# Where TensorE computes six value products ahead of the scores loop

## Chip, cores and metric

The kernel runs on one core of a Trainium2 chip. The metric is the device time of one execution in microseconds (us). Several executions are timed, and one is profiled. Engines are named as in the profile: PE is TensorE's matmul, PEld its weight load, DVE VectorE, ACT ScalarE, POOL GpSimd, and SP the engine that issues most DMAs.

## The reference

A decoder layer on x (2048 x 256) and a context of 1601 x 256, all float32:

```
x = layernorm(x + linear_attention(x))            # 8 heads of 64; softmax of q over the head, of k over the tokens
x = layernorm(x + cross_attention(x, context))    # 16 heads of 16: softmax(Q K^T / 4) V, then Wo; biases on all
x = layernorm(x + moe(x) + shared(x))             # 16 experts of 128, the top 4 by a softmax gate
```

The change concerns the cross attention's V = context @ Wv, which the code calls the values: 13 blocks of 128 keys (the last of 65), each a 128 x 256 result.

## The kernel before, in words

The kernel is written for five engines by hand: each engine has its own instruction list, and semaphores order them. Three stages matter here.

**The front** (`for i in range(FRONT)`, 24 turns) computes the first attention for 16 tiles of tokens, turns the result, and computes the cross attention's queries. From turn 13 on it also carries two *units* a turn.

**A unit** (`max_unit`, matmuls on L1389) computes scores of 128 queries against 512 keys for one pair of heads (both sides in two banks of PSUM), only so that DVE can take their maximum (`read_max`, a reduction on L1853, or L1849 for the units of the remaining keys). A group of 4 heads and 512 queries has 26 units: 24 full ones and two of the remainder (8 matmuls of 66 keys each), the last of which is unit 25. When the last unit of a group is read, DVE forms the group's negated maxima (`finish_max`, L1893 and L1897), SP writes them to DRAM and reads them back into a row of the stacked queries (`stack_max`, L602 and L606), and only then may the true scores of that group be computed. Units alternate between two places in PSUM, so unit u waits until unit u - 2 is read (`max_read` at u - 1). Units 0 to 21 stand in the front's turns. Units 22 to 29 follow in a loop of their own, the *lead*; units 26 to 29 belong to group 1.

**The scores loop** (208 steps: 4 chunks of 512 queries x 4 groups x 13 key blocks). A step issues two units, four scores (L1465, which ACT turns into probabilities on L1210), and the weighing of the values for the step two before (L1479). Before the first unit of the loop, unit 30, there stand waits for the copies of values 0 to 10 and for the reads of group 0; before the first scores, a wait for group 0's row of maxima.

**A value** (`value(t)`, L1350) is four matmul instructions of 256 columns with four weight loads on PE, into bank 2 or 3 of PSUM by turns; ACT copies it out (`copy_values`, L1047) and POOL adds the bias (`add_value_bias`, L908), each in the order of t. Value t waits for the copy of value t - 2 (the last, 12, for that of 11). Values 0 to 5 are computed in the front, value 12 inside step 0 of the loop, and values 6 to 11 in the lead. Before the change value 6 stands behind unit 26, 7 behind 27, 8 behind 28, 9 behind 29, and 10 and 11 behind that. POOL clears a buffer behind its last bias addition (L948). ACT and POOL have no order between values and units: they take the values as they come.

Names and lines: `UNITS_IN_LOOP` = 22, `UNITS` = 26, `PER_STEP * LEAD` = 30, `VALUES_IN_LEAD` = 6 to 11; `value` L1339, `max_unit` L1362 on, the lead L1697 to L1703, the waits ahead of the loop L1704 to L1706, the loop from L1707; `query` products of the cross attention are on L1439, their copies on L1067 and L1068.

Of the kernel before, what the change touches and what calls it, by code (L numbers as in the profile page):

```python
# [46 lines left out]
UNITS = TPC * PAIRS * MAIN + PAIRS  # L47
PER_STEP = UNITS // KT
LEAD = KT + 2
# [8 lines left out]
UNITS_IN_LOOP = 2 * (FRONT - FIRST_UNIT_AT)  # L58
# [72 lines left out]
def krows(kt):  # L131
    return P if kt < KT - 1 else LASTK
# [12 lines left out]
def decoder_layer(nc, a, out):  # L145
    with ExitStack() as ctx:
# [20 lines left out]
        def bank(n, w=1):  # L167
            return psum[:, n * CHUNK:(n + w) * CHUNK]
# [203 lines left out]
        def units_until(step):  # L372

            return min(CHUNKS * GROUPS * UNITS, PER_STEP * (step + 1 + LEAD))
# [53 lines left out]
        VALUES_AT = {2: (0, 1, 2), 19: (3,), 20: (4,), 23: (5,)}  # L428
        VALUES_IN_HEAD = 3
        VALUES_IN_LEAD = range(6, KT - 1)  # L430
        VALUES_CLEARED_AT = 15
        BIASED_AT = {19: (0,), 20: (1,), 21: (2,), 22: (3,), 23: (4,)}
        BIASED_BEHIND = range(5, KT)
        assert sorted(sum(VALUES_AT.values(), ()) + tuple(VALUES_IN_LEAD)) == list(range(KT - 1))

        def vals_bank(t):
            return 5 + t if t < VALUES_IN_HEAD else 3 if t == KT - 1 else 2 + t % 2
# [89 lines left out]
        def _(sp):  # L527
# [151 lines left out]
            def name_tiles(v):  # L679


                n = min(EXPERT_LOAD, SLOT_TILES - v)
                sp.wait_ge(order_in, 16)
                _, got = nc.values_load_multi_w_load_instructions(
                    order_row[0:1, 0, v:v + n, 1], engines=[mybir.EngineType.SP], min_val=0, max_val=SLOT_TILES - 1,
                    skip_runtime_bounds_check_because="the order is a permutation of the tiles")
                for k in range(n):
                    tile_at[v + k] = got[k]
# [92 lines left out]
        def _(pool):  # L781
# [136 lines left out]
            for i in range(FRONT):  # L918
                if XQ_RING <= i + 1 < TILES:
                    split_query_tile(i + 1)  # L920
                if i < KEY_PLACES - CLEARED_FIRST:
                    pool.memset(kstack[:, CLEARED_FIRST + i, :].bitcast(F32), 0.0).then_inc(keys_cleared, 1)
                if i == VALUES_CLEARED_AT:
                    pool.memset(region1[:, KW:KW + VALS].rearrange("p (n w) -> p n w", w=VW)[:, :, C_DH:VW], 1.0
# [90 lines left out]
        def _(act):  # L1015
# [28 lines left out]
            def copy_values(t):  # L1044
                r = krows(t)
                act.wait_ge(vc_ready, t + 1)
                act.activation(vals[0:r, :, t, :, 0:C_DH],  # L1047
                               bank(vals_bank(t))[0:r, 0:DIM].rearrange("p (g h d) -> p g h d", g=GROUPS, h=GROUP),
                               ACT.Copy).then_inc(vc_copied, 1)
# [4 lines left out]
            for i in range(FRONT):  # L1054
# [40 lines left out]
                for t in vals_at(i):  # L1095
                    copy_values(t)
            for t in VALUES_IN_LEAD:
                copy_values(t)
# [156 lines left out]
        def _(pe):  # L1255
# [38 lines left out]
            for t in range(TILES + 2):  # L1294
# [8 lines left out]
                if t >= 2:  # L1303
                    u = t - 2
# [34 lines left out]
            def value(t):  # L1339
                if t == 0:  # L1340
                    pe.wait_ge(kc_copied, 2)
                elif t == VALUES_IN_HEAD:
                    pe.wait_ge(y_read, TILES)
                elif t == VALUES_IN_HEAD + 1:
                    pe.wait_ge(qT_copied, TILES)
                elif t > VALUES_IN_HEAD:
                    pe.wait_ge(vc_copied, t if t == KT - 1 else t - 1)
                r = krows(t)
                for k in range(DK):
                    mm = pe.matmul(bank(vals_bank(t))[0:r, 0:DIM], ctxT[:, k, t * P:t * P + r], wv_c[:, k, :],  # L1350
                                   start=(k == 0), stop=(k == DK - 1))
                mm.then_inc(vc_ready, 1)
# [41 lines left out]
            for i in range(FRONT):  # L1394
# [5 lines left out]
                t = i - ATTEND  # L1400
# [8 lines left out]
                t = i - TURN_X  # L1409
# [11 lines left out]
                t = i - TURN_Q  # L1421
# [274 lines left out]

            in_lead = iter(VALUES_IN_LEAD)  # L1697
            for u in range(UNITS_IN_LOOP, units_until(-1)):
                max_unit(u)
                if u >= UNITS:  # L1700
                    value(next(in_lead))
            for t in in_lead:
                value(t)  # L1703
            pe.wait_ge(vc_copied, KT - 2)  # L1704
            pe.wait_ge(y_read, TILES)
            pe.wait_ge(max_read, UNITS)  # L1706
# [718 lines left out]
```

## Time and profile before

| | us |
|---|---|
| median of 3 timed runs | 945.13 (944.79 to 947.65) |
| the profiled execution, its own time | 943.31 |
| its span in the profile | 941.5 |
| mean granted clock of TensorE over the span | 0.991 |
| PE busy | 890.7 (95%) |
| DVE busy | 709.4 (75%) |
| ACT busy | 662.1 (70%) |
| POOL busy | 309.8 (33%) |

The profile is of one execution, and times in it count from the start of its span. The lead lies between 175 and 191 us. In a timeline row the first number is the start, the second the duration of the merged instructions, and the bracket says how long the engine stood idle before them and what ended that. The granted clock is a share of the full 2.4 GHz: 1.00 is that, 0.50 is 1.2 GHz.

### The profile page before, as it was taken

How to read it: one execution, taken by the hardware profiler on the slowest of the kernel's cores; microseconds unless marked ns; L12 is line 12 of the kernel's file. 1: busy time of each engine (PE TensorE's matmuls, PEld its weight loads, DVE VectorE, ACT ScalarE, POOL GpSimd, SP SyncE). 2: the span in 40 equal slices, each digit the busy share in tenths (PEclk: the TensorE clock that was granted, in tenths of full speed). 3: DMA queues.
4: the chain of work that ended last, by engine and by line, in shares of the span. 5: the costliest groups of instructions: out<-in, count | busy, mean ns of one | idle time of the engine just before them, and what ended most of it. 6: DMA issues, size and time to landing. Idle time of an engine off the chain costs nothing.

```text
span 941.5 us, 18997 instructions
## 1 busy us (share of the span) xinstructions
PE 890.7 (95%) x6843; PEld 506.4 (54%) x6843; DVE 709.4 (75%) x1140; ACT 662.1 (70%) x1489; POOL 309.8 (33%) x360
## 2 busy tenths in 40 slices
PE   9999999899999999999999999999989997799995
PEld 5776775444444444444444444444433486577783
DVE  5337788789999998989998989997897272311487
ACT  4435764278888888888888888876779763466664
POOL 1916887430000000110000200013544446555674
PEclk9999999899999999999999999999999999999998
DMA  9208439203343400100100100102345443345695
GB/s 326 83 1 153 113 108 160 86 7 98 95 144 105 129 17 24 28 11 25 31 8 24 30 9 25 31 19 86 101 128 159 120 129 119 120 133 167 245 305 188
DMA packets 69779, 91.53 MB, mean 97 GB/s; under 512 B 15224, under 2 KB 52602, under 8 KB 69656
## 3 DMA queue, kind: packets, MB, share of 16 engines
q1 hardware_dynamic: 62008, 68.52, 25.8%
q0 software_dynamic: 6928, 18.82, 5.4%
q10 hardware_dynamic: 752, 2.98, 1.9%
q8 instruction: 56, 0.92, 0.4%
q14 instruction: 35, 0.29, 0.1%
HBM read 48.80 MB, written 39.40 MB: 94 GB/s over the span
## 4 chain that ended last, share of the span: by engine, by line
PE 79%; DVE 13%; ACT 4%; issue 3%; DMA 1%; another core or an unknown queue 0%; POOL 0%; POOLq 0%; DVEq 0%; SPq 0%; ACTq 0%
PE psum L1479 20%; PE psum L1389 16%; PE psum L1465 10%; PE psum L1663 9%; DVE mpart L1853 7%; PE psum L1681 4%; PE psum L1309 2%; PE psum L1274 2%; PE psum L1625 2%; PE psum L1439 2%; PE psum L1406 2%; PE psum L1501 1%; PE psum L1282 1%; ACT region L1075 1%; PE psum L1350 1%
## 5 line engine op out<-in xcount | busy, mean ns | idle before, releaser
L1210 ACT ACTIVATE region<-psum 128x512 f32<-128x512 f32 (+1 forms) x832 | 448.1, 606 | 84.8 <-PE psum L1465 68.7
L1853 DVE TENSOR_REDUCE mpart<-psum 128x2 f32<-128x1024 f32 x384 | 462.1, 1221 | 33.8 <-PE psum L1389 27.1
L1479 PE MATMUL psum<-region 128*32 128x256 f32 (+1 forms) x3120 | 248.8, 391 | 2.2 <-ACT numT L1106 0.6
L1389 PE MATMUL psum<-kstack,qstack 63*128 63x512 f32 (+1 forms) x1024 | 212.0, 442 | 10.8 <-DVE mpart L1853 8.5
L1389 PEld LDWEIGHTS psum<-kstack,qstack 63*128 63x128 f32 x1024 | 88.4, 184 | 179.7 <-issue 127.9
L1465 PE MATMUL psum<-qstack,kstack 64*128 64x512 f32 (+1 forms) x832 | 175.6, 407 | 1.3 <-ACT region L1210 0.8
L1479 PEld LDWEIGHTS psum<-region 128*32 128x32 f32 (+1 forms) x3120 | 62.3, 108 | 111.0 <-issue 83.4
L1465 PEld LDWEIGHTS psum<-qstack,kstack 64*128 64x128 f32 (+1 forms) x832 | 111.2, 181 | 18.0 <-ACT region L1210 11.1
L956 POOL TENSOR_TENSOR attnT<-num_c,den_c 128x512 f32<-128x512 f32 x7 | 9.0, 1284 | 309.6 <-DMA den_c<-den_d 309.5
L887 POOL DMA_INDIRECT given_d<-y_out,x_in x79 | 77.8, 984 | 60.3 <-ACT y_out L1182 41.9
L2223 DVE SCALAR_TENSOR_TENSOR act_h<-silu_h,psum 128x128 f32<-128x128 f32 x95 | 27.1, 286 | 89.5 <-ACT silu_h L1164 49.7
L1663 PE MATMUL psum<-w_all,xT_in 128*128 x316 | 83.5, 387 | 7.7 <-DVE act_h L2223 5.9
L1663 PEld LDWEIGHTS psum<-w_all,xT_in 128*128 128x128 f32 x316 | 53.8, 190 | 16.5 <-issue 12.3
L850 POOL DMA_INDIRECT sorted_d<-x_rows,slots x48 | 47.4, 987 | 34.9 <-PE psum L1465 24.5
L1164 ACT ACTIVATE silu_h<-psum 128x128 f32<-128x128 f32 x85 | 24.5, 288 | 40.4 <-PE psum L1663 28.4
L1681 PE MATMUL psum<-w_all,actT 128*128 x158 | 47.4, 382 | 1.5 <-ACT y_out L1182 1.5
L1160 ACT ACTIVATE xT_in<-psum 128x256 f32<-128x256 f32 x95 | 37.1, 391 | 13.9 <-PE psum L1625 11.4
L1075 ACT ACTIVATE region<-psum,small 128x64 f32<-128x64 f32 x128 | 27.9, 329 | 26.8 <-DVE small L1864 26.7
L1182 ACT ACTIVATE y_out<-psum,x_in 128x256 f32<-128x256 f32 x79 | 38.2, 484 | 11.7 <-PE psum L1681 6.7
L1849 DVE TENSOR_REDUCE mpart<-psum 128x8 f32<-128x528 f32 x32 | 22.5, 707 | 12.0 <-PE psum L1389 10.3
L1174 ACT ACTIVATE actT<-psum 128x128 f32<-128x128 f32 x95 | 27.3, 287 | 5.3 <-PE psum L1671 3.0
L1625 PE MATMUL psum<-ident,x_in 128*128 128x128 f32 x158 | 30.5, 275 | 0.5 <-issue 0.3
(298 smaller groups left out, 1008.0 us busy)
## 6 DMA issues: line engine op xcount, KB each, us to landing
x_in<-sorted_d SPq DMA_DIRECT2D x79, 129.0 KB
sorted_d<-x_in SPq DMA_DIRECT2D x6, 1548.0 KB, 7.9
given<-given_d SPq DMA_DIRECT2D x16, 512.0 KB
qstack<-qparts_d SPq DMA_DIRECT2D x96, 64.0 KB, 2.3
qparts_d<-region SPq DMA_DIRECT2D x8, 512.0 KB, 3.0
kparts_d<-region SPq DMA_DIRECT2D x4, 800.5 KB, 9.7
kstack<-kparts_d SPq DMA_DIRECT2D x6, 400.2 KB, 10.0
kstack<-kparts_d ACTq DMA_DIRECT2D x6, 400.2 KB, 13.4
```

Source lines behind the costliest of these rows:

```text
L850: pool.indirect_dma_start(out=sorted_d[:, :], out_offset=bass.IndirectOffsetOnAxis(ap=slots[:, t, j:j + 1], axis=0), in_=row, in_offset=No ...
L887: pool.indirect_dma_start(out=given_d[:, :], out_offset=bass.IndirectOffsetOnAxis(ap=x_in[:, v % X_SLOTS, DIM:DIM + 1].bitcast(I32), axis= ...
L1075: ins = act.activation(qexp[:, i % 2, head], bank(i % 2)[:, head], ACT.Exp, bias=small[:, 32 * (i % 2) + h:32 * (i % 2) + h + 1])
L1182: act.activation(y_out[:, v % Y_SLOTS, :], bank(2 + i % 2)[:, 0:DIM], ACT.Copy, scale=x_in[:, v % X_SLOTS, DIM + 1:DIM + 2]).then_inc(y_co ...
L1210: act.activation(prob[0:rows_of, s % 3, j, :], ring(n)[0:rows_of], ACT.Exp).then_inc(ring_read, 1)
L1389: mm = pe.matmul(bank(unit_bank(u) + side)[:, at * w:(at + 1) * w], qstack[rows_of, buffer(G), p, t * P:(t + 1) * P], kstack[rows_of, g * ...
L1465: pe.matmul(ring(n)[0:r], kstack[rows, g * PAIRS + p, kt * P:kt * P + r], qstack[rows, buffer(G), p, :], start=True, stop=True).then_inc(r ...
L1479: mm = pe.matmul(bank(NUM_BANK)[VW * j:VW * (j + 1), q], vals[0:r, g, kt, j, :], prob[0:r, s % 3, j, q], start=(kt == 0 and half == 0), st ...
L1625: mm = pe.transpose(turn_bank("tile", i)[:, k * P:(k + 1) * P], rows[:, k * P:(k + 1) * P], ident[:, :])
L1663: mm = pe.matmul(bank(6 + i % 2)[:, 0:2 * HID], xT_in[:, i % 3, k * P:(k + 1) * P], part_of(kind, v, k), start=(k == 0), stop=(k == DK - 1))
L1681: pe.matmul(bank(2 + i % 2)[:, 0:DIM], actT[:, i % ACT_SLOTS, :], part_of(kind, v, DK), start=True, stop=True).then_inc(y_done, 1)
L1853: dve.tensor_reduce(mpart[:, G % 2, qt, :, p, n], both, X, ALU.max).then_inc(max_read, 1)
```

## The change

A tuple names the units behind which the six values of the lead stand: 22 and 23 (the first two behind the front's loop), 25 (the last of the remainder), and 26, 27 and 28 (the first three of group 1). The lead's loop takes the next value behind each of them, and the loop over what is left falls away. The same six values are computed by the same instructions, in the same order among themselves, with the same waits. ACT, POOL, DVE and SP have the same lists as before.

```diff
@@ -428,10 +428,12 @@
         VALUES_IN_LEAD = range(6, KT - 1)
+        VALUE_BEHIND_UNIT = (UNITS_IN_LOOP, UNITS_IN_LOOP + 1, UNITS - 1, UNITS, UNITS + 1, UNITS + 2)
...
+        assert len(VALUE_BEHIND_UNIT) == len(VALUES_IN_LEAD) and max(VALUE_BEHIND_UNIT) < PER_STEP * LEAD
@@ -1697,10 +1699,8 @@
             in_lead = iter(VALUES_IN_LEAD)
             for u in range(UNITS_IN_LOOP, units_until(-1)):
                 max_unit(u)
-                if u >= UNITS:
+                if u in VALUE_BEHIND_UNIT:
                     value(next(in_lead))
-            for t in in_lead:
-                value(t)
             pe.wait_ge(vc_copied, KT - 2)
```

## Rows read from the trace of the kernel before

**Rows 1.** The page: busy time of the engines, and the chain that ended last.
```profile
PE 890.7 (95%) x6843; PEld 506.4 (54%) x6843; DVE 709.4 (75%) x1140; ACT 662.1 (70%) x1489; POOL 309.8 (33%) x360
...
PE 79%; DVE 13%; ACT 4%; issue 3%; DMA 1%; another core or an unknown queue 0%; POOL 0%; POOLq 0%; DVEq 0%; SPq 0%; ACTq 0%
```

**Rows 2.** Stretch of the loop: PE, PEld, DVE, ACT, POOL busy, clock, DMA share, GB/s.
```profile
190.00:300.00 110.00, 109.07 (x1056) 49.57 (x1054) 103.05 (x94) 95.06 (x178) 8.22 (x7) 1.00 0.31 95
```

**Rows 3.** The same columns for three stretches ahead of the loop.
```profile
166.40:169.80 3.40, 2.21 (x9) 1.05 (x8) 3.40 (x4) 0.12 (x1) 2.73 (x5) 1.00 0.33 124
...
176.40:180.30 3.90, 1.76 (x18) 1.23 (x19) 3.78 (x5) 0.00 (x0) 1.66 (x3) 1.00 0.36 134
180.40:187.20 6.80, 6.80 (x16) 3.74 (x17) 3.87 (x6) 0.77 (x2) 1.45 (x2) 0.50 0.17 47
```

**Rows 4.** Timeline of PE, from value 5 to unit 32.
```profile
174.38 1.13 PE L1350 MATMUL psum<-region 128*128 128x256 f32 x4
175.44 0.82 PE L1389 MATMUL psum<-kstack,qstack 63*128 63x512 f32 x4
177.26 0.49 PE L1389 MATMUL psum<-kstack,qstack 63*128 63x512 f32 x2 [1.00 <-DVE mpart L1853]
178.39 0.63 PE L1389 MATMUL psum<-kstack,qstack 63*128 63x66 f32 x8 [0.63 <-DVE mpart L1853]
179.52 0.63 PE L1389 MATMUL psum<-kstack,qstack 63*128 63x66 f32 x8 [0.50 <-DVE mpart L1853]
180.32 0.78 PE L1389 MATMUL psum<-kstack,qstack 63*128 63x512 f32 x2 [0.17 <-issue]
181.04 2.07 PE L1350 MATMUL psum<-region 128*128 128x256 f32 x4
183.04 0.79 PE L1389 MATMUL psum<-kstack,qstack 63*128 63x512 f32 x2
...
188.31 2.86 PE L1350 MATMUL psum<-region 128*128 128x256 f32 x12
191.10 0.50 PE L1389 MATMUL psum<-kstack,qstack 63*128 63x512 f32 x2
191.44 0.40 PE L1465 MATMUL psum<-qstack,kstack 64*128 64x512 f32 x2
191.67 0.40 PE L1389 MATMUL psum<-kstack,qstack 63*128 63x512 f32 x2
...
192.51 0.50 PE L1465 MATMUL psum<-qstack,kstack 64*128 64x512 f32 x1 [0.23 <-ACT region L1210]
...
193.96 0.50 PE L1389 MATMUL psum<-kstack,qstack 63*128 63x512 f32 x2
```

**Rows 5.** Timeline of DVE in the same stretch.
```profile
175.98 3.49 DVE L1853 TENSOR_REDUCE mpart<-psum 128x2 f32<-128x1024 f32 x3 [0.26 <-PE psum L1389]
...
181.33 1.18 DVE L1853 TENSOR_REDUCE mpart<-psum 128x2 f32<-128x1024 f32 x1
...
191.64 2.36 DVE L1853 TENSOR_REDUCE mpart<-psum 128x2 f32<-128x1024 f32 x2 [2.00 <-PE psum L1389]
```

**Rows 6.** Timeline of ACT: the copy of value 6, and the first exponential.
```profile
183.15 0.38 ACT L1047 ACTIVATE region<-psum 128x256 f32<-128x256 f32 x1 [7.21 <-PE psum L1350]
...
191.86 0.60 ACT L1210 ACTIVATE region<-psum 128x512 f32<-128x512 f32 x1 [0.27 <-PE psum L1465]
```

**Rows 7.** DMA issues of SP for the row of maxima, and landing times of the stacked queries' DMAs.
```profile
181.44 0.65 SPq L602 DMA_DIRECT2D max_d<-negT  x1
183.50 0.54 SPq L606 DMA_DIRECT2D qstack<-max_d  x2
...
DMA to landing us min/median/max: 2.0/2.2/2.3
```

**Rows 8.** PE's timeline and a stretch's row, around the pause before 791.48.
```profile
791.48 2.05 PE L1663 MATMUL psum<-w_shared,xT_in 128*128 128x256 f32 x4 [3.87 <-issue]
...
792.00:793.00 1.00, 1.00 (x4) 0.78 (x3) 0.45 (x2) 1.00 (x5) 0.00 (x0) 0.50 0.00 0
```

## Prediction

> **What bounds the kernel now.** I read the page first: TensorE (PE) is busy for 95% of the span and carries 79% of the chain that ended last, VectorE (DVE) 13% of it [rows 1]. Then the busy times by stretch. From 190 to 300 us, the scores loop, PE is busy for 109.07 of 110 us and DVE for 103.05 [rows 2]: whatever moves the start of that loop on both engines moves the end of the kernel. Ahead of it there is a stretch that looks different. From 176.4 to 180.3 PE is busy for only 1.76 of 3.90 us while DVE is busy for 3.78; from 180.4 to 187.2 PE is busy throughout, but at a granted clock of 0.50, which is the lower of its two levels, 1.2 GHz; from 166.4 to 169.8 PE was less than full too (2.21 of 3.40), and the clock stayed at 1.00 [rows 3].
>
> The timeline of PE says what these are [rows 4]. Unit u is one pass of L1389. Value 5 starts at 174.38 behind unit 20, the merged row at 175.44 is units 21 and 22, then come 23 (177.26), 24 (178.39), 25 (179.52) and 26 (180.32), each behind an idle gap: 1.00, 0.63, 0.50 and 0.17 us. The first three end with a reduction of DVE, since a unit waits until all but the last unit before it are read; DVE runs there almost without a break (three reads in 3.49 us from 175.98, [rows 5]). So the place is DVE-bound, with PE empty. From 181.04 (value 6) on it is the other way round: values 6, 7, 8 behind units 26, 27, 28, unit 29, then values 9, 10, 11 in a row (one row of 12 matmuls, 2.86 us), and unit 30, the first of the loop, at 191.10. Here PE sets the pace and DVE waits (2.00 us before its read at 191.64, rows 5 again).
>
> **The change, part by part.** Nothing is added or removed: 24 matmuls of six values (four each) with their weight loads change place. No DMA is issued by them and none is passed on PE's queue. A value of four takes 1.06 us at the full clock between units (value 5) and 0.93 where three stand together (2.79 from 188.31 to unit 30, a third each); I take 1.0. At the lower clock one takes 2.00 (181.04 to 183.04). A unit takes 0.41 to 0.43 at full clock (two in 0.82 from 175.44) and 0.72 at the lower (unit 26 at 180.32 to value 6 at 181.04) [rows 4]. The new order is 22, v6, 23, v7, 24, 25, v8, 26, v9, 27, v10, 28, v11, 29, loop. Step by step at full clock:
> - v6 behind unit 22: 176.3 to 177.3. Unit 23 was let go at 177.26. Cost nil; the cover is the 1.00 us gap, without which it would cost 1.0.
> - v7 behind unit 23 (177.7 to 178.7): unit 24 starts at about 178.75 instead of 178.39. DVE reads 22 and 23 until 179.4 (175.98 + 3.49), so its next read, that of unit 24, is not late, and unit 25, which waits for read 23, stays at 179.52. Cost nil, with 0.1 us to spare at DVE.
> - v8 behind unit 25: 180.1 to 181.1, unit 26 at 181.1 instead of 180.32. Delay 0.8. DVE, free at 181.33 behind the two small operations of the maximum [rows 5], reads unit 26 at 181.6: 0.3 late.
> - Units 26 to 29 with v9, v10, v11 between: four units of 0.43 and three values of 1.0, 4.7 us, so unit 30 at 185.8. DVE keeps up: reads of 1.23 end at 182.9 (26), 184.3 (27) and 185.7 (28), and unit 30 needs the last of these.
> Before, unit 30 started at 191.10: 5.3 us less.
>
> The moved values' waits: each waits for ScalarE's copy of the value two before it. A copy starts 0.11 us behind the value and takes 0.38 (183.15, [rows 6]); a unit and a whole value lie between, so these waits cost nothing. The wait ahead of the loop is for the copy of v10 and is covered by 28, v11, 29. POOL's bias additions and its clearing behind them follow the copies to an earlier time, and nothing reads them before the third step.
>
> What is late next? Two things. The first scores of the loop wait for the row of maxima, by two DMAs of SP: issued at 181.44 and, when that has landed, at 183.50 and 0.54 us long; the first hop took 2.06, comparable pieces 2.0 to 2.3 [rows 7]. So the row is in at about 186.1. Scores stand 0.34 behind unit 30 (191.10 to 191.44, in the trace), now at 186.1 as well: cost nil, though the slack of 5 us is gone. Second, unit 31 waits for the read of unit 29: 185.9 + 1.23 = 187.15, where by the old spacing (191.67, 0.57 behind unit 30) it would stand at 186.4. The two scores behind it leave at 187.2 and 187.65; the last one was itself bound by ScalarE's first exponential (0.60 us, started 191.86, [rows 6]) at 1.41 behind unit 30 (192.51), so 0.45 us is lost there. Bounds: 0 (it catches up) and 0.75 (the whole wait). Value 12 and unit 32 follow: 189.1 against 193.96. DVE, which waited until 191.64 for its read of unit 30 [rows 5], will read it at 187.2 and have units 31 and 32 at hand behind it. Both engines enter the loop 4.9 us ahead, so neither can give it back by itself.
>
> **The sum.** Of the 5.3 us, the lower clock makes 3.3: the work from 180.32 to 188.31 (four units, three values) took 8.0 and would take 4.7. The other 2.0 is idle time filled, of the 2.3 that the four gaps hold. 5.3 less 0.45 is 4.9. The profiled execution took 943.31 us (span 941.5): it would be 938.4. The median of the runs is 1.8 above that execution: 945.13 - 4.9 = 940.2. About 0.3%, or 2.8 us, is what a measurement of this kernel can tell from no change.
>
> The sum needs the clock to stay up. Filled with v6, v7 and v8, the stretch of 1.76 busy us in 3.90 becomes some 3.9, more than that of 166.4 to 169.8, which let the clock stand at 1.00 [rows 3]. That is why I take it as staying.
> The trace shows one other fall while PE has work, after a pause of 3.87 us before 791.48, with 0.50 granted at 792 [rows 8]. The fall at 180.3 came with no pause above 1.00 us, only with several short ones.
> The Trainium skill, page "TensorE: Matmul & The Clock Gate", section "HAM oscillation", tells of a clock that is lost in long pauses, by which filling short gaps would save nothing of the clock and the sum would be that of rival 1, 943.7. Its next section has a kernel in which many short pauses did it, and by that the sum stays 940.2. The trace's fall at 180.3 agrees with the second, the one at 791 with the first.
>
> **Rivals.**
> 1. *The clock falls all the same at 180.3* and comes back at 187.2. For: what the chip looks at isn't the busy share that the profile shows, and the gaps of 166 to 170 stay. Then v8 is at 182.0, 26 and v9 end at 184.7, 27 and v10 at 187.4, 28, v11 and 29 at 189.3: unit 30 gains 1.8, less 0.45, some 1.4 in all: 943.7. Chance 0.12.
> 2. *The timed runs of before have no such fall.* One profiled execution shows it. Then only the filled gaps are left, 2.0 - 0.45 = 1.6: 943.5. Chance 0.12. The timed runs (944.79 to 947.65) spread by 2.9 us, which is of the size of this fall, but they carry no clock. The same page of the Trainium skill says, in Part 1, that the moment of a change of clock varies between runs of one kernel; no run here shows it yet.
> 3. *The row of maxima lands late.* If the second hop takes 4 us instead of 2, the first scores stand at 188.1 and 2 us of the gain are gone: 942.2. Chance 0.05; against it, both hops carry little and nothing else moves.
> 4. *Slower.* The place is PE's stretch from 173.96 to unit 30. If the clock falls early, at the gaps of 166.4 to 169.8 (2.21 of 3.40 us busy, [rows 3]), and stays down to the loop, then all that is packed there runs at half rate: from 176.3 to 185.8 there are 9.5 us of work at full clock, 8.5 of it by units and values, and it takes some 8 us more, with unit 30 near 193.9: 2.8 later, 948. It decides from 5.3 us of extra half-rate time on. Against it: in the trace the clock stands through 166 to 180 with more gaps than will be left. Chance 0.04.
> 5. *It does nothing,* because the advance is absorbed in the loop by a wait that isn't tied to its start. I find none: all that PE, DVE and SP wait for there is counted from the loop's own steps. 945.1, chance 0.02.
>
> **The numbers.** Forecast 0.65, 940.2, its own range 938.6 to 941.6 (delay terms of 0 to 0.8, a value at 0.93 or 1.06, runs that differ by a us). The range of 8 in 10 must reach rivals 1 to 3, hence up to 943.8, and down to 938.4. Faster by over 0.3% (below 942.3): the forecast and half of rival 3, 0.67. Within: rivals 1, 2, 5 and the rest of 3, 0.28. Slower: 0.05.
>
> **What would show it.** Right: between 176 and 186 PE has no gap above 0.3 us and a granted clock of 1.00; six values of about 1.0 us; unit 30 at 185.8 in place of 191.10; DVE busy nearly without a break from 174.5; the read of unit 29 as what ends the wait of unit 31; a shift of 4.9 us unchanged at 300 and at 700 us. Wrong: a granted clock of 0.50 anywhere from 170 to 200; unit 25 later than 179.6 (then v7 did cost DVE time); first scores released by the DMA of the maxima; a shift that shrinks inside the loop.

## The result, and the profile after

The changed kernel takes 939.97 us (median of 7 runs, 938.94 to 942.02) against 945.13 us (median of 7, 944.03 to 947.65) for the kernel before: a ratio of 0.9948, 95% interval 0.9931 to 0.9965. By the ratio that is 4.9 us less, 3.3 to 6.5, so clear of no change. The profiled execution took 940.66 us with a span of 938.9, against 943.31 and 941.5.

The page has the same instructions as before and nearly the same busy times; the first row answers to the first of [rows 1].

```profile
PE 891.0 (95%) x6843; PEld 506.1 (54%) x6843; DVE 709.6 (76%) x1140; ACT 663.2 (71%) x1489; POOL 310.8 (33%) x360
```

So the totals say nothing. The stretches do. Busy time by engine, granted clock and DMA, as in [rows 2] and [rows 3], of the changed kernel:

```profile
166.40:169.80 3.40, 2.22 (x9) 0.87 (x10) 3.40 (x4) 0.32 (x1) 2.91 (x5) 1.00 0.38 142
...
176.40:180.30 3.90, 3.75 (x29) 2.58 (x27) 3.90 (x4) 0.77 (x2) 3.26 (x5) 1.00 0.36 134
180.40:187.20 6.80, 6.58 (x28) 3.68 (x28) 5.65 (x7) 1.75 (x5) 2.93 (x4) 1.00 0.17 43
190.00:300.00 110.00, 109.44 (x1082) 49.17 (x1080) 105.14 (x96) 95.90 (x178) 5.97 (x4) 1.00 0.32 95
```

From 176.4 to 180.3 PE is busy for 3.75 us instead of 1.76, and from 180.4 to 187.2 its clock is 1.00 instead of 0.50. The stretch of 166.4 to 169.8, which the change doesn't touch, is as it was in this execution. The timeline of PE answers to [rows 4] (lines of this kernel are two higher: units on L1391, values on L1352, scores on L1467):

```profile
174.15 0.50 PE L1391 MATMUL psum<-kstack,qstack 63*128 63x512 f32 x2
...
175.65 0.82 PE L1391 MATMUL psum<-kstack,qstack 63*128 63x512 f32 x4
176.40 1.13 PE L1352 MATMUL psum<-region 128*128 128x256 f32 x4
177.47 0.49 PE L1391 MATMUL psum<-kstack,qstack 63*128 63x512 f32 x2
177.89 1.13 PE L1352 MATMUL psum<-region 128*128 128x256 f32 x4
178.96 1.41 PE L1391 MATMUL psum<-kstack,qstack 63*128 63x66 f32 x16
180.30 1.13 PE L1352 MATMUL psum<-region 128*128 128x256 f32 x4
181.36 0.49 PE L1391 MATMUL psum<-kstack,qstack 63*128 63x512 f32 x2
...
185.82 0.92 PE L1391 MATMUL psum<-kstack,qstack 63*128 63x512 f32 x4
186.56 0.42 PE L1467 MATMUL psum<-qstack,kstack 64*128 64x512 f32 x2
187.65 0.49 PE L1391 MATMUL psum<-kstack,qstack 63*128 63x512 f32 x2 [0.68 <-DVE mpart L1853]
...
188.31 1.08 PE L1352 MATMUL psum<-region 128*65 128x256 f32 x4
189.32 0.50 PE L1391 MATMUL psum<-kstack,qstack 63*128 63x512 f32 x2
```

Unit 20 starts at 174.15, units 21 and 22 at 175.65, then value 6, unit 23, value 7, units 24 and 25 in one row, value 8, unit 26 (181.36), and so on to units 29 and 30 in one row at 185.82, the first scores at 186.56, unit 31 at 187.65 and unit 32 at 189.32. The three gaps of 1.00, 0.63 and 0.50 us are gone, and the only row that still shows PE waiting for DVE is that of unit 31. (The row of units 24 and 25 hides one short pause between the two: the same 16 matmuls take 1.41 us here, and 1.08 in a kernel further down in which unit 25 has nothing to wait for.) Since the front ends at slightly different times in each execution, I measure from unit 20 to unit 32: 193.96 - 173.96 = **20.00 us before, 189.32 - 174.15 = 15.17 us after**. Everything the change does lies between these two.

The timeline of DVE, of which the first row answers to the first of [rows 5]:

```profile
176.19 3.49 DVE L1853 TENSOR_REDUCE mpart<-psum 128x2 f32<-128x1024 f32 x3 [0.27 <-PE psum L1391]
179.63 1.49 DVE L1849 TENSOR_REDUCE mpart<-psum 128x8 f32<-128x528 f32 x2
...
186.37 14.61 DVE L1853 TENSOR_REDUCE mpart<-psum 128x2 f32<-128x1024 f32 x12 [0.27 <-PE psum L1391]
```

It reads on without a break into the remainder's units at 179.63, so value 7 cost it nothing, and from 186.37 it reads without a break up to 200 us, where this view ends.

Is the advance kept? Each group of the loop ends with one copy of its weighed sum on ACT (L1106 before, L1108 after), which makes a good marker. ACT's timeline at group 0 and group 14, first in the kernel before:

```profile
227.93 0.60 ACT L1106 ACTIVATE numT<-psum 128x512 f32<-128x512 f32 x1
...
720.18 0.60 ACT L1106 ACTIVATE numT<-psum 128x512 f32<-128x512 f32 x1 [0.87 <-PE psum L1479]
```

and the changed one:

```profile
223.24 0.60 ACT L1108 ACTIVATE numT<-psum 128x512 f32<-128x512 f32 x1
...
716.02 0.60 ACT L1108 ACTIVATE numT<-psum 128x512 f32<-128x512 f32 x1 [0.87 <-PE psum L1481]
```

The advance is 4.69 us at group 0, between 4.60 and 4.76 at each of the groups up to 13, 4.16 at group 14 and 4.20 at the last, group 15. Behind the loop, in the experts' stage, whose work is the same in both kernels, the two profiled executions part by the clock: before, it was 0.83 on average from 786 to 796 and 1.00 from 812 to 820; after, 0.62 from 786 to 795 and 0.72 from 812 to 818, which is about 10 us at 0.50 instead of 3.4. The kernel before had about 10 us of it too in one of its two further executions and 3.4 in the other, so this varies without the change; whether the change has any part in it is not shown. The two spans differ by only 2.6 us where the loops' ends differ by 4.2. The timed runs show 4.9.

### The profile page after: what moved, and what is told of

Read it like the earlier page. It is cut to its first block, busy times and chain, and to the rows that moved or that the text cites. A ratio compares the mean times of both kernels' runs of the same rounds, so it can differ in the third digit from the quotient of the medians.

```text
span 938.9 us, 18997 instructions
## 1 busy us (share of the span) xinstructions
PE 891.0 (95%) x6843; PEld 506.1 (54%) x6843; DVE 709.6 (76%) x1140; ACT 663.2 (71%) x1489; POOL 310.8 (33%) x360
## 4 chain that ended last, share of the span: by engine, by line
PE 74%; DVE 14%; ACT 5%; issue 3%; DMA 2%; another core or an unknown queue 1%; POOL 0%; SPq 0%; POOLq 0%; DVEq 0%; ACTq 0%
PE psum L1481 20%; PE psum L1391 16%; PE psum L1467 9%; DVE mpart L1853 8%; PE psum L1665 7%; PE psum L1683 4%; PE psum L1311 2%; PE psum L1276 2%; ACT region L1212 2%; PE psum L1627 2%; PE psum L1441 2%; PE psum L1408 2%; PE psum L1503 1%; PE psum L1284 1%
## 5 line engine op out<-in xcount | busy, mean ns | idle before, releaser
L1391 PE MATMUL psum<-kstack,qstack 63*128 63x512 f32 (+1 forms) x1024 | 211.2, 441 | 9.4 <-DVE mpart L1853 7.2
L1391 PEld LDWEIGHTS psum<-kstack,qstack 63*128 63x128 f32 x1024 | 88.1, 184 | 178.6 <-issue 129.1
L1467 PE MATMUL psum<-qstack,kstack 64*128 64x512 f32 (+1 forms) x832 | 175.2, 407 | 1.0 <-DMA qstack<-max_d 0.5
L1467 PEld LDWEIGHTS psum<-qstack,kstack 64*128 64x128 f32 (+1 forms) x832 | 111.0, 181 | 17.5 <-ACT region L1212 11.9
L1665 PE MATMUL psum<-w_all,xT_in 128*128 x316 | 85.4, 394 | 6.6 <-DVE act_h L2223 4.9
L1408 PE MATMUL psum<-region 128*128 128x256 f32 x128 | 30.8, 384 | 0.0
## 6 DMA issues: line engine op xcount, KB each, us to landing
kstack<-kparts_d SPq DMA_DIRECT2D x6, 400.2 KB, 10.2
```

What stands on the lines that cost most here:

```text
L1391: mm = pe.matmul(bank(unit_bank(u) + side)[:, at * w:(at + 1) * w], qstack[rows_of, buffer(G), p, t * P:(t + 1) * P], kstack[rows_of, g * ...
L1408: mm = pe.matmul(bank(3)[:, 0:DIM], qsT[:, t % 2, f * P:(f + 1) * P], fold[:, f, :], start=(f == 0), stop=(f == SF - 1))
L1467: pe.matmul(ring(n)[0:r], kstack[rows, g * PAIRS + p, kt * P:kt * P + r], qstack[rows, buffer(G), p, :], start=True, stop=True).then_inc(r ...
L1665: mm = pe.matmul(bank(6 + i % 2)[:, 0:2 * HID], xT_in[:, i % 3, k * P:(k + 1) * P], part_of(kind, v, k), start=(k == 0), stop=(k == DK - 1))
```

## The experiments

There are ten runs: the kernel before twice more, the changed one once more, and seven other kernels. Four of them (the two of before, one value early, and the cover taken away) have a single timed run, so a profile and no ratio. Where ratios are given, they are to runs of the kernel before in the same session. The kernels with extra work compute a value product one time too many into a bank of PSUM that is free, and nobody reads it (called a filler); the outputs are the same. "20 to 32" stands below for the time from the start of unit 20 to that of unit 32.

### The kernel before, two more times

Unchanged, to see whether the fall of the clock is a property of the kernel.

> The kernel before, unchanged, to see whether its clock falls at the same place in another execution. Theory (the thin stretch of 176.4 to 180.3 us lets the clock fall): a granted clock of 0.50 for some 6.8 us beginning within 177 to 184 us, values behind units 26 to 28 of about 2.0 us each, unit 32 at 193.5 to 194.5. Rival (the fall at 180.3 was particular to the one execution that was profiled): clock 1.00 from 170 to 200, all values about 1.0 us, unit 32 near 190.7, and then only the filled gaps, some 1.6 us, are a lasting gain of the change.

> The kernel before a third time. Two executions of it had a fall of the clock behind unit 25, of 6.8 and of some 4 us, with 20.00 and 18.48 us from unit 20 to unit 32. Theory (the thin stretch lets the clock fall, where and for how long differs between executions): a fall again that begins between 168 and 184, and 17.5 to 20.2 us from unit 20 to unit 32. Rival (a fall there is chance, not of the thin stretch): no fall from 165 to 200 and 17.0 us.

PE's timeline in the first of these (the lines of code are those of before), with units 25 and 26 in the first row and values 6, 7 and 8 behind units 26, 27 and 28:

```profile
179.56 1.27 PE L1389 MATMUL psum<-kstack,qstack 63*128 63x66 f32 x10 [0.50 <-DVE mpart L1853]
180.76 1.74 PE L1350 MATMUL psum<-region 128*128 128x256 f32 x4
182.43 0.79 PE L1389 MATMUL psum<-kstack,qstack 63*128 63x512 f32 x2
183.15 1.81 PE L1350 MATMUL psum<-region 128*128 128x256 f32 x4
184.89 0.50 PE L1389 MATMUL psum<-kstack,qstack 63*128 63x512 f32 x2
185.32 1.13 PE L1350 MATMUL psum<-region 128*128 128x256 f32 x4
```

and stretches of the second, in the columns of [rows 2]:

```profile
176.40:180.30 3.90, 1.76 (x18) 1.23 (x18) 3.81 (x4) 0.00 (x0) 1.77 (x3) 1.00 0.36 134
181.00:191.00 10.00, 10.00 (x25) 5.82 (x24) 5.25 (x7) 1.15 (x3) 2.18 (x3) 0.52 0.18 55
```

The thin stretch is the same to 0.01 us in each, and behind it the clock fell each time, but for a different time: 6.8 us in the profile before, 3.4 in the first of these (from 181.1 to 184.6: the first two values take 1.7 us each instead of 2.0, the third 1.06), and 10.2 in the second (from 180.4 to 190.6). "20 to 32" was 20.00, 18.48 and 21.54 us. So the fall is the kernel's, and its length is the execution's. Both expectations had the fall right and its length too narrow: 6.8 us and unit 32 at 193.5 or later were expected of the first, which had 3.4 us and 192.46; at most 20.2 us of the second, which took 21.54. The spread of 3.1 us in this one place compares with one of 5.9 and 5.2 us among the 16 and 19 timed runs of before in the two sessions.

The rival that the timed runs of before have no such fall is answered by more than these three executions, since each timed run has its mean granted clock on record. In the session of the second of these profiles it is 0.987 on average over the 19 runs of before, and 0.991 over the 10 of the changed kernel. By my estimate (0.9908 - 0.9869, times 944 us) that is 3.7 us less lost to the lower clock, give or take 1.6 (95%). The mean can't say where in the kernel it is lost; its size is that of the fall.

### The clock's part by itself: fillers in the gaps

The order of before, and PE computes value 6 without use behind units 22, 23 and 25.

```diff
+            def filler(t):
+                pe.wait_ge(vc_copied, t - 1)
+                for k in range(DK):
+                    pe.matmul(bank(vals_bank(t))[:, 0:DIM], ctxT[:, k, t * P:(t + 1) * P], wv_c[:, k, :],
+                              start=(k == 0), stop=(k == DK - 1))
...
             for u in range(UNITS_IN_LOOP, units_until(-1)):
                 max_unit(u)
+                if u in (UNITS_IN_LOOP, UNITS_IN_LOOP + 1, UNITS - 1):
+                    filler(6)
                 if u >= UNITS:
                     value(next(in_lead))
```

> The order of before, with one extra value product (four matmuls of 256 columns, value 6 computed one time too many and not copied) behind each of units 22, 23 and 25. PE's gaps are filled with work that nobody needs, so the clock's part is measured by itself. Theory: the clock stays at 1.00, unit 30 at about 188.8 and unit 32 at 191.7, 2.3 us before the 193.96 of before (3.3 for the clock, less about 0.8 for the filler behind unit 25 and 0.2 besides), time 943 or so. Rival (the gain of the change is filled idle time alone, or the clock falls for another reason): clock 0.50 from about 180 to 187 all the same, unit 32 at 194.8, 0.8 us later than before.

PE's timeline in this kernel; the fillers are L1700:

```profile
177.77 1.13 PE L1700 MATMUL psum<-region 128*128 128x256 f32 x4
...
181.67 1.13 PE L1700 MATMUL psum<-region 128*128 128x256 f32 x4
...
183.16 1.13 PE L1350 MATMUL psum<-region 128*128 128x256 f32 x4
...
190.44 0.50 PE L1389 MATMUL psum<-kstack,qstack 63*128 63x512 f32 x2
```

and two stretches of it, in the columns of [rows 2], where the kernel before stood at 0.50:

```profile
182.00:184.00 2.00, 2.00 (x10) 1.23 (x8) 1.65 (x4) 0.00 (x0) 0.00 (x0) 1.00 0.00 0
184.00:186.00 2.00, 2.00 (x10) 1.05 (x8) 1.73 (x2) 0.56 (x2) 0.73 (x1) 1.00 0.06 10
```

The clock stayed at 1.00 from 174 to 200 and the values behind units 26, 27 and 28 took 1.06 us each. "20 to 32" was 193.30 - 175.52 = 17.78 us, 2.22 less than the 20.00 of before where 2.3 was expected, and the timed ratio is 0.9971 (0.9952 to 0.9989): **a kernel that does more work is 2.7 us faster** (1.0 to 4.5). The mean clock of its timed runs is 0.990, against 0.987 for before in the same session. This settles the rival that the gain is filled idle time alone, since nothing useful was moved here. With 0.85 us for the filler behind unit 25 (unit 26 stands 7.21 us behind unit 20, and 6.36 before), the order of before would take 16.9 to 17.0 us at full clock. That is an estimate; one value early, below, gives 17.1 by another way: 16.02 us without a fall, and the 1.06 of its one value that the gap hides. With 17.0, the falls cost 3.0, 1.5 and 4.5 us in the three executions of before, and the change gains 17.0 - 15.17 = 1.8 us besides.

This execution also showed a fall that I had only allowed for: the clock was at 0.50 for 3.4 us from 169.1 on, and unit 20 stood at 175.52 instead of about 174.1. So this one profile can't rule out that the earlier fall had a part in there being none later; the timed runs don't depend on it. More on it below.

### One value in the gaps, and two

The tuple names unit 22 alone, or 22 and 23, ahead of group 1; the other values stand behind units 26 to 29, and what is left behind those. The edit for one value, against the kernel before:

```diff
         VALUES_IN_LEAD = range(6, KT - 1)
+        VALUE_BEHIND_UNIT = (UNITS_IN_LOOP, UNITS, UNITS + 1, UNITS + 2, UNITS + 3)
...
-                if u >= UNITS:
+                if u in VALUE_BEHIND_UNIT:
                     value(next(in_lead))
             for t in in_lead:
```

> Value 6 alone stands in a gap (behind unit 22); 7, 8, 9 stand behind units 26, 27, 28, value 10 behind 29 and value 11 behind that. PE's idle time between 176 and 180.3 falls from 2.3 to 1.3 us. If that is enough to keep the clock: unit 32 at about 190.0, 4 us earlier than before. If the clock still falls at 180.3: unit 32 at about 193.0, 0.9 us earlier, the one value's worth. The theory doesn't say which, and the run measures it; a result between the two would speak for a fall at another time.

> Values 6 and 7 stand in the gaps (behind 22 and 23); 8 to 11 behind units 26 to 29. Theory: value 8 behind unit 25 in the change only swaps its place with a value ahead of unit 30, since PE is never idle from unit 26 on: the clock stays at 1.00, unit 26 starts at 180.3 instead of 181.1, and unit 32 is within 0.3 us of that of the changed kernel (189.1 on the clock of before's trace), time 940.0 to 940.8. Rival (the third value is needed to keep the clock up, or to fill idle time): unit 32 at 190 or, with a fall, at 192.

With one value early the gaps ahead of units 24 and 25 are as wide as before. PE's timeline (lines one higher than before), with units 24 and 25 (unit 26 is merged into the second row) and the next value:

```profile
178.52 0.63 PE L1390 MATMUL psum<-kstack,qstack 63*128 63x66 f32 x8 [0.64 <-DVE mpart L1854]
179.65 1.27 PE L1390 MATMUL psum<-kstack,qstack 63*128 63x66 f32 x10 [0.50 <-DVE mpart L1854]
180.85 1.13 PE L1351 MATMUL psum<-region 128*128 128x256 f32 x4
```

No fall: the clock is 1.00 up to 200 us, and "20 to 32" is 190.10 - 174.08 = 16.02 us, which is 4.0 earlier than before, the first of the two outcomes named. In this one execution, filling the single gap of 1.00 us was enough for the clock. With two it is 15.24 us, 0.07 more than with the change's three, and the timed ratio is 0.9948 (0.9932 to 0.9964), the change's own. So value 8 behind unit 25 does nothing: it puts off unit 26 by as much as it saves further on. In these single profiles most of the gain hangs on the first value moved; the second is worth 0.8.

### The changed kernel again

> The changed kernel a second time. Theory: from unit 20 to unit 32 it takes 15.2 us as in the first profile (15.17), with the clock at 1.00 from 174 on; a fall that the gaps of 166 to 172 bring about may end in 168 to 174, before the change's place, and then moves unit 20, not the 15.2. Rival (the clock falls in the lead in some executions of this kernel too): 0.50 somewhere from 176 to 190 and 17 us or more.

PE's timeline in the last turns of the front, up to unit 20:

```profile
168.77 3.52 PE L1441 MATMUL psum<-xT,region 128*128 128x512 f32 x4
172.22 0.84 PE L1391 MATMUL psum<-kstack,qstack 63*128 63x512 f32 x4
173.74 1.95 PE L1441 MATMUL psum<-xT,region 128*128 128x512 f32 x4 [0.68 <-ACT region L1070]
175.63 0.50 PE L1391 MATMUL psum<-kstack,qstack 63*128 63x512 f32 x2
```

"20 to 32" is 15.16 us, the first profile's 15.17, and the ratio of the timed runs is 0.9953 (0.9939 to 0.9967). But here the clock fell behind the gaps of 166 to 168, for 3.4 us from 169.1 on: a query product (L1441) took 3.52 us instead of 1.98, and unit 20 started 1.5 us late. That is the third execution with this fall, of nine whose front has the order of before (this one, the fillers in the gaps, two values early). The change doesn't touch it. When it happened, no fall followed behind unit 25, but all three were kernels with filled gaps there. So these three say less than the others on whether filled gaps keep the clock.

### The cover taken away

One more filler between unit 22 and value 6 in the changed kernel.

```diff
                 max_unit(u)
+                if u == UNITS_IN_LOOP:
+                    filler(6)
                 if u in VALUE_BEHIND_UNIT:
```

> The changed kernel with one more product of no use (four matmuls, 1.06 us) between unit 22 and value 6, so that the gap of 1.00 us that hides value 6 is overfilled. Theory (the gaps are DVE's time, and PE has 1.0 + 0.63 + 0.50 to give away between unit 22 and unit 26, of which the three values have taken nearly all): unit 23 about 1.0 later than in the changed kernel, unit 26 about 0.75 later, and 15.9 to 16.2 us from unit 20 to unit 32 instead of 15.17. Rival (PE has more room than that, since the reads go on behind): unit 32 less than 0.3 later. Rival (the maxima of group 0, which come with unit 25, then hold up the first scores): the first scores wait for the DMA qstack<-max_d and unit 32 is more than 1.1 later.

PE's timeline: the filler (L1702), value 6, unit 23, and further down units 26 and 32:

```profile
176.23 1.13 PE L1702 MATMUL psum<-region 128*128 128x256 f32 x4
177.20 1.03 PE L1352 MATMUL psum<-region 128*128 128x256 f32 x4
178.16 0.49 PE L1391 MATMUL psum<-kstack,qstack 63*128 63x512 f32 x2
...
181.72 0.50 PE L1391 MATMUL psum<-kstack,qstack 63*128 63x512 f32 x2
...
189.69 0.49 PE L1391 MATMUL psum<-kstack,qstack 63*128 63x512 f32 x2
```

Counted from unit 20 (173.98 here), unit 23 stands at 4.18 instead of 3.32, unit 26 at 7.74 instead of 7.21, unit 32 at 15.71 instead of 15.17. The pair of products together took 1.93 us rather than twice 1.06, and of that 0.86 showed at unit 23 and 0.54 at the end. The direction was right, all three amounts came out lower than the 1.0, 0.75 and at least 0.7 that I had written. Most of that is the first, the extra product showing as 0.86; between units 23 and 26 some 0.33 us were taken up where I had counted 0.25. They are the pause ahead of unit 25: units 24 and 25 take 1.08 us here and 1.41 in the changed kernel. The first scores weren't held up by the DMA of the maxima.

### Two steps earlier, with and without fillers, and one step

Could more be had by moving all values further forward? Two steps: values 5, 6, 7 in turns 21, 22, 23 of the front.

```diff
-        VALUES_AT = {2: (0, 1, 2), 19: (3,), 20: (4,), 23: (5,)}
-        VALUES_IN_LEAD = range(6, KT - 1)
-        VALUE_BEHIND_UNIT = (UNITS_IN_LOOP, UNITS_IN_LOOP + 1, UNITS - 1, UNITS, UNITS + 1, UNITS + 2)
+        VALUES_AT = {2: (0, 1, 2), 19: (3,), 20: (4,), 21: (5,), 22: (6,), 23: (7,)}
+        VALUES_IN_LEAD = range(8, KT - 1)
+        VALUE_BEHIND_UNIT = (UNITS_IN_LOOP, UNITS_IN_LOOP + 1, UNITS - 1, UNITS)
```

> The changed kernel with values 5, 6, 7 in turns 21, 22, 23 of the front (before: 5 in turn 23), and 8 to 11 behind units 22, 23, 25 and 26; nothing stands between units 27 to 30. Theory: from 174 us on DVE's reductions set the pace, so that PE has nothing more to win: units 28 to 31 each wait for a read, unit 31 starts within 0.4 us of where it does in the changed kernel, unit 20 up to 0.4 later (value 6 in turn 22 is only partly hidden), DVE without idle time above 0.3 from 175 to 187, and the time equals that of the changed kernel within 1 us. Rival (PE is the bound up to unit 30, and two values fewer there are 2.1 us): unit 32 some 2 us earlier than in the changed kernel.

PE's timeline: units 27 and 28 in one row, units 29, 30 and 31, and value 12:

```profile
183.49 0.83 PE L1391 MATMUL psum<-kstack,qstack 63*128 63x512 f32 x4
185.32 0.49 PE L1391 MATMUL psum<-kstack,qstack 63*128 63x512 f32 x2 [1.00 <-DVE mpart L1853]
186.54 0.50 PE L1391 MATMUL psum<-kstack,qstack 63*128 63x512 f32 x2 [0.73 <-DVE mpart L1853]
...
187.58 0.80 PE L1391 MATMUL psum<-kstack,qstack 63*128 63x512 f32 x2 [0.29 <-DVE mpart L1853]
...
188.73 1.97 PE L1352 MATMUL psum<-region 128*65 128x256 f32 x4
```

and the stretch behind that, in the columns of [rows 2]:

```profile
187.20:197.00 9.80, 9.51 (x40) 4.22 (x40) 6.17 (x6) 5.71 (x11) 4.79 (x3) 0.50 0.14 36
```

My expectation was right on three of the four waits (units 29, 30 and 31 wait for reads, unit 28 doesn't) and on where unit 31 starts, and missed what the waits would bring: where nothing stands between units 27 and 30, the gaps of 1.00, 0.73 and 0.29 us are a thin stretch like the old one in a new place, and the clock fell behind it, from 187.1 to 197.4 us, inside the loop. Group 0 ended at 227.10 instead of 223.24, and the timed ratio to before is 0.998 (0.9965 to 0.9995), about 2.6 us worse than the 0.9953 of the changed kernel in the same session; equal times within 1 us were expected. The profiled execution, though, was the slowest of its ten (948.3 us, the median is 945.13), and the mean clock of the ten is 0.990, hardly under the changed kernel's 0.991. So a fall of 10 us is not shown to be what the other nine had, and part of the 2.6 us stays unexplained. Fillers behind units 27 and 28 of this kernel then test whether the gaps did it:

```diff
                 if u in VALUE_BEHIND_UNIT:
                     value(next(in_lead))
+                if u in (UNITS + 1, UNITS + 2):
+                    filler(10)
```

This filler waits until value 10 is copied (`vc_copied` at t + 1), since it uses the same bank.

> The kernel with the values two steps earlier, whose clock fell at 187 and stood at 0.50 for 10 us, with one product of no use behind each of units 27 and 28, where PE waited 1.00, 0.73 and 0.29 us for DVE. Theory (a stretch in which PE waits for the reads makes the clock fall, and the 10 us at half rate were the loss): the clock stays at 1.00 from 174 to 200, the work added costs at most 0.5 us in its gaps, the end of group 0's weighing (the first copy of numT) comes at about 223.6 instead of 227.1, and the time is 0.3% below that of the same kernel without filler, ratio to before 0.995. Rival (the fall came from something else, or was chance of one execution): group 0 ends no earlier than 227, and the timed ratio stays at 0.998 or grows by the added work.

The same stretch in this kernel:

```profile
187.20:197.00 9.80, 8.97 (x72) 3.85 (x73) 9.64 (x9) 7.88 (x16) 4.80 (x3) 1.00 0.11 36
```

The clock was 1.00 from 160 to 200, and group 0 ended at 223.92, 3.2 us earlier than without the fillers (223.6 was expected). The timed ratio of 0.9968 (0.9948 to 0.9989) missed the 0.995 I had written and overlaps that of the kernel without fillers (0.998): in the timed runs the gain isn't shown, only in the trace. That fits a fall that doesn't happen, or not as long, in every execution, as does the mean clock above, but there is one profile of each. That the fillers kept the clock is seen in one execution, and what it is worth in the timed runs is open.

One step: 5 in turn 21, 6 in turn 23, then 7, 8, 9 behind units 22, 23, 25, 10 behind 26 and 11 behind 28.

> The changed kernel with every moved value one place earlier: 5 in turn 21 of the front, 6 in turn 23, 7, 8, 9 behind units 22, 23, 25, then 10 behind 26 and 11 behind 28, none behind 27. Theory (DVE's reads are the bound there and at most 0.4 us is to be won): group 0's weighing ends at 222.9 to 223.7 if the clock stays, against 223.24 in the changed kernel, and the ratio to before is 0.994 to 0.996, no better than the change within what can be told. Risk, by the theory: PE waits up to 0.7 us before units 28 and 30, and if that is thin enough the clock falls as it did with two steps: group 0 then ends 3 us later. Rival (PE is still the bound and a value fewer is 1 us): 222.2.

PE's timeline at unit 30:

```profile
186.03 0.50 PE L1391 MATMUL psum<-kstack,qstack 63*128 63x512 f32 x2 [0.72 <-DVE mpart L1853]
```

The waits were 0.72 us ahead of unit 30 and 0.31 ahead of unit 31, the clock stayed at 1.00, "20 to 32" took 14.56 us, and group 0 ended at 222.85, 0.4 before the changed kernel's. The timed ratio is 0.9951 (0.9933 to 0.997), no different from the change's. DVE's reads are the bound there, as said, and the change has taken nearly all that there was.

## Why the prediction was right

The forecast of 940.2 us (4.9 less) came out as 939.97, a ratio worth 4.9. The mechanism is shown: with the gaps filled the clock stays up, and the loop keeps the advance. That the number is so close is in part luck, as the fifth and sixth points say. The steps, in the order of the prediction:

- **v6 costs nothing.** Unit 23 starts 3.32 us behind unit 20 (3.30 before). Right.
- **v7 costs DVE nothing, and unit 24 about 0.36.** Unit 24 starts 4.81 us behind unit 20 instead of 4.43, and DVE runs on. Right.
- **v8 puts off unit 26 by 0.8.** 7.21 us behind unit 20 instead of 6.36, so 0.85. Right, and the experiment with two values shows that it buys nothing.
- **Unit 30 5.3 us earlier.** The first scores stand at 186.56, so by the old distance of 0.34 unit 30 is at 186.22, 12.07 behind unit 20 against 17.14: 5.1 us. The values take 1.06 us each here, where I had 1.0; four of them make the 0.2.
- **0.45 lost at unit 31.** The wait is there (0.68 us, ended by DVE). But between units 30 and 32 only 3.10 - 2.86 = 0.24 us were lost: the two scores behind unit 31 left in one row of 0.39 us, where I had put 0.45 between them. The two small errors cancel: 15.14 was forecast from unit 20 to unit 32, 15.17 measured.
- **3.3 us for the clock, 2.0 for filled gaps.** The fillers put the clock's part at 3.0 in the profiled execution, and the filled gaps at 1.8 net, or 2.1 with the 0.24 of unit 31 added back. The 3.3 was taken from one execution, and it was 1.5 and 4.5 in the two others. That the execution profiled first had the middle of the three is luck: from the shortest fall, the same working would have given a gain of some 3.4 us, from the longest 6.4, and a forecast of 941.7 or 938.7.
- **The row of maxima isn't late.** The first scores follow unit 30 at the old distance. Right, also 0.4 us earlier still, with values one step earlier.
- **The loop passes the advance on.** Right to 0.1 us up to group 13, then half a microsecond less, which the prediction had named as a sign of being wrong. At group 14 PE waits for the row of maxima in both kernels (0.46 us before, 0.49 after, DMA of qstack), so it isn't a new wait. Nor does it follow the change: from the end of group 11 to that of group 14 the three executions of before took 115.6, 116.0 and 116.4 us, the two of the changed kernel 116.1 and 116.6, so the first profile of before is the one that was quick there.
- **The clock at 1.00 from 170 to 200.** Another sign of being wrong was 0.50 anywhere in there. The first profile of the changed kernel has none. The second has it from 169.1 to 172.5, ahead of the change's place and in gaps that the change leaves open, so the risk that rival 4 named exists, though it cost 1.5 us and not 8.

Of the rivals, the first (the clock falls all the same) was refuted: in nine profiled executions with work in the gap behind unit 22 the clock never fell between 174 and 187 us, where all three of before fell. Only the kernel with two steps fell behind that, at its new gaps. Three of the nine had had the earlier fall; the other six stand without that doubt. The second fell with the repeats and with the mean clock of the timed runs, the third with the first scores, the fifth with the markers in the loop. The fourth, slower by a clock that is low for longer, didn't come true for the change. Two steps earlier, more than half of the gain was gone in the timed runs, and the profile shows such a fall, at new gaps that the removal of values makes further on; the rival had named only those of 166 to 168.

On the long-pause rule of the Trainium skill, page "TensorE: Matmul & The Clock Gate", section "HAM oscillation", the runs are clear for this place: the longest pause ahead of the fall was 1.00 us, three executions fell, and filling the pauses with idle work kept the clock. The next section of that page of the Trainium skill, "A second HAM failure mode", where frequent short pauses did it, is the one that agrees. The statement of the Trainium skill in Part 1 of the same page, that the moment of a change varies between runs of one kernel, agrees too: the clock came back at 187.2, 184.6 and 190.6 us in the three executions of before.

## What to carry to other kernels

Where TensorE waits for a reader in short gaps, look at the granted clock of the stretch that follows: the gaps may cost more afterwards than they are long (here 1.5 to 4.5 us behind 2.1 us of gaps), and independent work moved into them can pay twice. Work that is moved out of a place leaves that place thin, so follow the gaps to their new home before moving more. A place in which the clock falls for different times must be judged by several profiles or by timed runs, and a marker pair around it (here units 20 and 32) shows in tenths of a microsecond what the whole time shows in whole ones.

## What the runs showed of the hardware that I hadn't expected

- The same stretch of the same kernel, the same to 0.01 us in PE's busy time, was followed by 6.8, 3.4 and 10.2 us at the lower clock in three executions, with PE busy throughout (10.00 of 10 us in the longest).
- Filling one gap of 1.00 us was enough to keep the clock, with gaps of 0.64 and 0.50 us left open (one execution).
- The gaps of 166 to 168 us, with 2.2 of 3.4 us busy, were followed by 3.4 us at the lower clock in three of nine executions, where I had read from one trace that the clock stands there.
